# A four-stage transformer kernel: a re-ordered, deeper feed-forward pipeline and moved slots in attention

## The chip, the cores and the metric

The kernel runs on one core of a Trainium2 chip. The metric is the device time of one execution in microseconds (us). The engines are TensorE (PE; PEld is its weight load), VectorE (DVE), ScalarE (ACT), GpSimd (POOL) and SyncE (SP), which issues the DMAs. TensorE's clock has two levels, 1.2 and 2.4 GHz; a granted clock of 1.00 means all of a stretch at the upper one.

## The reference

The input is x of 16 x 256 tokens, 128 features. Four blocks follow each other, each as x = layernorm(x + block(x)): a selective scan (Mamba), a feed-forward part with blockwise FP4 quantization, a differential attention, and a three-layer part with +-1 weights. The change touches the second and the third.

```python
def fp4_quant_dequant(x):            # blocks of 16 along the last dimension
    scale = jnp.maximum(jnp.max(jnp.abs(xb), axis=-1, keepdims=True) / 6.0, 1e-12)
    idx = jnp.searchsorted(_MID, jnp.abs(xb / scale))
    return _GRID[idx] * jnp.sign(xb / scale) * scale
# feed-forward, hidden size 352; x and h are quantized, and the weights too
h = silu(fp4_linear(x, w_gate)) * fp4_linear(x, w_up)
y = fp4_linear(h, w_down)
# attention: q, k rotated; 8 heads with two maps each (16 maps), head dimension 8
o = sdpa(q1, k1, v) - lam * sdpa(q2, k2, v)
o = (o * rsqrt(mean(o**2) + eps) * ln_w + ln_b) * (1 - LAMBDA_INIT)
y = o @ Wo.T
```

## The kernel before

`x_all` keeps all 32 tiles of 128 tokens in SBUF. The stages run one after the other: `mamba_phase`, `ffn_phase`, `attention_phase`, `mlp_phase`. In each one every engine has its own instruction stream, written out by hand in order; semaphores tie them together. So an instruction that waits holds back everything behind it on its engine.

**Feed-forward** (`ffn_phase`). Eight groups of four tiles (512 tokens). A group passes: quantize x (DVE: block maximum, scale, reciprocal, correction, product, L122 to L130; ACT: absolute value, L816; DVE: "magic" maximum and product, L144; POOL: add and subtract the magic number, L149 and L151, which rounds; DVE: multiply by the scale, L156), turn x on PE (L909) and copy it (L847), gate and up projections per tile (L874, L875), silu (L823), product `hidden` (L753), quantize h the same way on 1408 columns instead of 512, turn h (L884), copy (L841, L843), residual (L897) and down projections (L890) into the PSUM tile `dn`, statistics (L81, L86), deviation on POOL (L799), shift (L770), normalize on ACT (L830). `body(n)` on each engine is one step. It mixes group n (gate, up, product, scaling of h), group n+1 (quantization of x) and group n-1 (h back-scaled, turned, projected down, statistics). The scales are in SBUF. Steps 0 to 8 or 9 run, 2 to 6 of them as a hardware loop (`blocks`).

**Attention** (`attention_phase`). One step handles one batch row's scores (two tiles, 16 maps), in 16 slots `u`. In each slot PE makes the scores of map u of group n (`scores`) and two maps' products for the row maximum of a later group (`maxima`), DVE takes the maximum (`row_max`, L1109), and ACT the exponential (L1296). `DELAY` says in which slot the first maximum of group n+2 falls. All other work of groups n-3 to n+5 is hung on slots. The chain that feeds q and k: rotate on POOL, turn on PE (slot 0, L1406), two copies on ACT (L1302, L1304), remainder on POOL (L1232), second part on ACT (L1313), third part on POOL (L1240), parts to DRAM by SP (L1063), back as rows of `qs` and `ks` (L1075, L1078; semaphore `q_in`), awaited by `maxima` with i = 0. The negative maxima are split in three by `split_max`, turned (L1423), copied (L1318, `nmT`) and sent as three rows of `qs` (L1067). SP issues, in this order: parts, the rows of maxima, the loads of q and k.

Of the kernel before, what the change touches and what calls it, by code (L numbers as in the profile page):

```python
# [21 lines left out]
P = 128  # L22
# [633 lines left out]
def ffn_phase(nc, k):  # L656
# [3 lines left out]

    HB = HID // QB
    HC = [(c * P, min(P, HID - c * P)) for c in range((HID + P - 1) // P)]
    ctx = ExitStack()
    with ctx:
# [10 lines left out]
        qh = Quant(sb, sem, "qh", GT * HB)  # L677
# [3 lines left out]
        xqT = sb("xqT", [P, GTOK])  # L681
        sg = sb("sg", [P, GT, HID])
        hid = sb("hid", [P, GT, HID])
        hqT = sb("hqT", [P, 2, len(HC), P])
        stats = sb("stats", [P, GT, 6])
        mv = sb("mv", [P, GT, 2])
        veps = sb("veps", [P, GT])
        rstd = sb("rstd", [P, GT])
# [4 lines left out]
        tx = ps("tx", [P, 512])  # L693
        th = [ps(f"th{i}", [P, 512]) for i in range(2)]
        dn = ps("dn", [P, GT, DM])

        w_turned = sem("w_turned")
        w_copied = sem("w_copied")
        x_turned = sem("x_turned")
# [3 lines left out]
        hid_ready = sem("hid_ready")  # L703
        h_turned = sem("h_turned")
        h_copied = sem("h_copied")
        down_ready = sem("down_ready")
        shift_ready = sem("shift_ready")
        stat_chain = sem("stat_chain")
        rstd_ready = sem("rstd_ready")
        norm_chain = sem("norm_chain")  # L710

        def blocks(eng, body, first=-1):
            for n in range(first, 2):
                body(n)
            with eng.Fori(2, GROUPS - 1) as n:
                body(n)
            for n in range(GROUPS - 1, GROUPS + 2):
                body(n)

        def has(n, lag):  # L720

            return not isinstance(n, int) or 0 <= n + lag < GROUPS
# [9 lines left out]

# [13 lines left out]
        @block.vector  # L746
        def _(dve):
            quant_back(nc, dve, qx, 0)

            def hidden(n, j):  # L750
                if has(n, 0):
                    dve.wait_ge(silu_ready, GT * n + j + 1)
                    nc.vector.tensor_tensor(hid[:, j], sg[:, j], up[j % 2][:, 0:HID], ALU.mult).then_inc(hid_ready, 1)  # L753

            def body(n):
                if has(n, 1):
                    quant_scale(nc, dve, k, qx, ffn_blocks(k, n + 1), n + 1)
                hidden(n, 0)
                if has(n, 1):
                    quant_magic(nc, dve, qx, n + 1)  # L760
                hidden(n, 1)
                hidden(n, 2)
                hidden(n, 3)
                if has(n, -1):
                    wait(dve, h_turned, GT * (n - 1))
                    quant_back(nc, dve, qh, n - 1)
                if has(n, -2):
                    m = n - 2
                    dve.wait_ge(rstd_ready, m + 1)
                    nc.vector.scalar_tensor_tensor(out=shift[:], in0=mv[:, :, 0], scalar=-1.0, in1=rstd[:],  # L770
                                                   op0=ALU.mult, op1=ALU.mult).then_inc(shift_ready, 1)
                if has(n, 0):
                    dve.wait_ge(hid_ready, GT * n + GT)
                    quant_scale(nc, dve, k, qh, hid[:].rearrange("p a (b e) -> p (a b) e", e=QB), n)
                if has(n, 1):
                    wait(dve, x_turned, n + 1)
                    quant_back(nc, dve, qx, n + 1)
                if has(n, 0):
                    quant_magic(nc, dve, qh, n)
                if has(n, -1):  # L780
                    m = n - 1
                    wait(dve, norm_chain, m)
                    dve.wait_ge(down_ready, GT * m + GT)
                    layer_norm_stats(dve, nc, dn, stats, mv, veps, stat_chain, 3 * m)
                    nc.vector.tensor_scalar(veps[:], mv[:, :, 1], LN_EPS, None, ALU.add).then_inc(stat_chain, 1)

            blocks(dve, body, 0)
            dve.wait_ge(norm_chain, GROUPS)

        @block.gpsimd  # L790
        def _(pool):
            def body(n):
                if has(n, 1):
                    quant_middle(nc, pool, qx, n + 1)
                if has(n, 0):
                    quant_middle(nc, pool, qh, n)
                if has(n, -1):
                    pool.wait_ge(stat_chain, 3 * (n - 1) + 3)
                    nc.gpsimd.tensor_tensor(rstd[:], veps[:], k.neg_half[:, 0:GT], ALU.pow).then_inc(rstd_ready, 1)  # L799

            blocks(pool, body, 0)

        @block.scalar
        def _(act):

            for n, dst in enumerate((wgT, wuT)):
                act.wait_ge(w_turned, n + 1)
                nc.scalar.activation(dst[:], (gp[0], up[0])[n][:, 0:HID], ACT.Copy).then_inc(w_copied, 1)
            act.wait_ge(w_turned, 3)
            for c, (_, rows) in enumerate(HC):  # L810
                last = nc.scalar.activation(wdT[0:rows, c, :], tx[0:rows, P * c:P * c + P], ACT.Copy)
            last.then_inc(w_copied, 1)

            def absolute(q, m):
                act.wait_ge(q.front, 6 * m + 5)
                nc.scalar.activation(q.magic[:], q.xs, ACT.Abs).then_inc(q.absolute, 1)  # L816

            def body(n):
                if has(n, 0):
                    for j in range(GT):  # L820
                        act.wait_ge(up_ready, GT * n + j + 1)
                        wait(act, hid_ready, GT * (n - 1) + j + 1)
                        nc.scalar.activation(sg[:, j], gp[j % 2][:, 0:HID], ACT.Silu).then_inc(silu_ready, 1)  # L823
                        if j == 0 and has(n, 1):
                            absolute(qx, n + 1)
                if has(n, -2):
                    m = n - 2
                    act.wait_ge(shift_ready, m + 1)
                    for j in range(GT):
                        last = nc.scalar.activation(k.x_all[:, bass.ds(GT * m + j, 1), :].rearrange("p a b -> p (a b)"),  # L830
                                                    dn[:, j], ACT.Identity, scale=rstd[:, j:j + 1], bias=shift[:, j:j + 1])
                    last.then_inc(norm_chain, 1)
                if has(n, 0):
                    absolute(qh, n)
                if has(n, -1):
                    for j in range(GT):
                        act.wait_ge(h_turned, GT * (n - 1) + j + 1)
                        wait(act, down_ready, GT * (n - 1) + j - 1)
                        src = th[j % 2][:, 0:len(HC) * P].rearrange("p (c t) -> p c t", c=len(HC))
                        full = len(HC) - 1  # L840
                        nc.scalar.activation(hqT[:, j % 2, 0:full], src[:, 0:full], ACT.Copy)  # L841
                        rows = HC[-1][1]
                        nc.scalar.activation(hqT[0:rows, j % 2, full], src[0:rows, full], ACT.Copy).then_inc(h_copied, 1)  # L843
                if has(n, 1):
                    act.wait_ge(x_turned, n + 2)
                    wait(act, up_ready, GT * (n + 1))
                    nc.scalar.activation(xqT[:], tx[:], ACT.Copy).then_inc(x_copied, 1)  # L847

            blocks(act, body)

        @block.tensor
        def _(pe):
# [8 lines left out]
            for c, (at, rows) in enumerate(HC):  # L861
                a = 2 * len(HC) * DM + at
                last = nc.tensor.transpose(tx[0:rows, P * c:P * c + P], wq[:, a:a + rows], ident)
            last.then_inc(w_turned, 1)
            pe.wait_ge(w_copied, 3)

            def body(n):
                if has(n, 0):
                    pe.wait_ge(x_copied, n + 1)
                    for j in range(GT):  # L870
                        wait(pe, silu_ready, GT * n + j - 1)
                        wait(pe, hid_ready, GT * n + j - 1)
                        xt = xqT[:, P * j:P * j + P]
                        nc.tensor.matmul(gp[j % 2][:, 0:HID], xt, wgT[:], start=True, stop=True)  # L874
                        nc.tensor.matmul(up[j % 2][:, 0:HID], xt, wuT[:], start=True, stop=True).then_inc(up_ready, 1)  # L875
                if has(n, -1):
                    m = n - 1
                    pe.wait_ge(qh.back, m + 1)
                    hq = qh.out.rearrange("p (a b) e -> p a (b e)", a=GT)

                    def turn(j):
                        wait(pe, h_copied, GT * m + j - 1)
# [1001 lines left out]
```

## Time and profile before

| | us |
|---|---|
| median of 3 runs (1236.98 to 1244.79) | 1238.01 |
| profiled execution, its own time | 1237.58 |
| its span | 1235.8 |
| PE / DVE / POOL / ACT busy in the span | 968.2 / 942.1 / 818.5 / 720.7 |
| mean granted clock | 0.894 |

The span counts from the first to the last instruction. Mamba fills it up to about 503 us, the feed-forward part up to about 703, attention up to about 1073, and the last part the rest. A busy share says how much an engine worked, not what held it up; for that one reads the waits and the timeline. Times in the timeline are from the span's start.

### The profile page before, as it was taken

The numbers are of one execution on the slowest core, as the hardware profiler recorded it, in microseconds if no ns is written. First come the engines' busy times: TensorE is split into PE (matmuls) and PEld (weight loads), VectorE is DVE, ScalarE is ACT, GpSimd is POOL, SyncE is SP. The second block draws the span as 40 slices with busy tenths as digits, with TensorE's granted clock in tenths as the row PEclk, the third lists the DMA queues.
The fourth block names the chain that finished last, engine by engine and source line by source line (L and its number), as shares of the span: only waits on it lengthen the run. The fifth ranks groups of instructions, "written<-read, shape, count | busy, mean of one in ns | idle before, by whom it ended". The sixth has DMA issues, their size and how long they took to land. (4 is left out here: it accounts for less than half of the span.)

```text
span 1235.8 us, 15659 instructions
## 1 busy us (share of the span) xinstructions
PE 968.2 (78%) x4332; PEld 486.8 (39%) x4347; DVE 942.1 (76%) x1625; ACT 720.7 (58%) x1406; POOL 818.5 (66%) x747
## 2 busy tenths in 40 slices
PE   5689797979797877466665548898898988489996
PEld 2233343424233322343443424454444543235553
DVE  3799999999999999566565226787677784359996
ACT  3777686868676653323333313776666667278772
POOL 1898989899999997244442354575847643467773
PEclk9899999989899989768787655999989999789998
DMA  5552534424251510600000023332323220000001
GB/s 175 229 240 91 195 128 169 172 103 173 102 207 68 228 47 1 108 15 1 0 0 0 1 80 88 91 105 63 95 64 92 79 79 2 0 1 10 18 9 34
DMA packets 34878, 103.84 MB, mean 84 GB/s; under 512 B 3627, under 2 KB 22443, under 8 KB 23979
## 3 DMA queue, kind: packets, MB, share of 16 engines
q1 hardware_dynamic: 34807, 103.03, 24.2%
q8 instruction: 28, 0.46, 0.1%
q14 instruction: 43, 0.35, 0.1%
HBM read 93.71 MB, written 8.91 MB: 83 GB/s over the span
## 5 line engine op out<-in xcount | busy, mean ns | idle before, releaser
L554 PE MATMUL m_yac<-m_hC,ident 128*128 128x512 f32 x512 | 266.5, 641 | 73.6 <-DVE m_hC L315 46.5
L506 POOL TENSOR_TENSOR m_dBu<-m_du,m_Bt 128x1024 f32<-128x1024 f32 x128 | 299.3, 2356 | 6.5 <-DVE m_dA L306 5.1
L1109 DVE TENSOR_REDUCE a_nm<-a_s 128x2 f32<-128x512 f32 x256 | 170.4, 686 | 95.3 <-PE a_s L1348 89.4
L306 DVE TENSOR_TENSOR_SCAN m_dA<-m_dA,m_dBu 128x512 f32<-128x512 f32 x184 | 221.7, 1219 | 15.1 <-ACT m_dA L444 12.1
L1296 ACT ACTIVATE a_pT<-a_s 128x512 f32<-128x512 f32 x256 | 150.9, 600 | 96.9 <-PE a_s L1348 95.9
L554 PEld LDWEIGHTS m_yac<-m_hC,ident 128*128 128x128 f32 x512 | 93.1, 198 | 225.5 <-issue 105.1
L444 ACT ACTIVATE m_dA<-m_delta,mprm 128x510 f32<-128x510 f32 x256 | 169.4, 675 | 0.3
L1348 PE MATMUL a_s<-ks,qs 72*128 72x256 bf16 x512 | 106.5, 294 | 33.0 <-DMA ks<-parts 22.7
L315 DVE TENSOR_TENSOR m_hC<-m_dA,m_Ct 128x512 f32<-128x512 f32 x184 | 123.3, 670 | 0.0
L516 POOL TENSOR_TENSOR m_hC<-m_hS,m_Ct 128x512 f32<-128x512 f32 x72 | 94.6, 1314 | 31.7 <-DVE m_hS L306 31.5
L1644 POOL TENSOR_TENSOR b_h_rest<-b_h_full,b_h_parts 128x512 f32<-128x512 f32 x64 | 77.2, 1212 | 44.9 <-ACT b_h_parts L1669 36.8
L441 ACT ACTIVATE m_dA<-m_zero 128x2 f32<-128x2 f32 x181 | 30.9, 171 | 127.1 <-DVE m_hC L315 126.8
L1348 PE MATMUL a_s<-qs,ks 99*128 99x256 bf16 x512 | 100.9, 281 | 3.2 <-ACT a_pT L1296 2.7
L306 DVE TENSOR_TENSOR_SCAN m_hS<-m_dA,m_dBu 128x512 f32<-128x512 f32 x72 | 86.8, 1206 | 0.0
L1693 PE MATMUL b_hp<-b_h_parts,b_w 128*128 128x512 bf16 x375 | 86.1, 383 | 0.7
L149 POOL TENSOR_TENSOR f_qh_q<-f_qh_xs,f_qh_magic 128x1408 f32<-128x1408 f32 x8 | 25.3, 3165 | 79.5 <-DVE f_qh_magic L144 79.5
L1348 PE MATMUL a_pv<-a_pT,vx 128*32 128x512 f32 x512 | 71.5, 633 | 0.7 <-ACT a_pT L1296 0.7
L1590 DVE TENSOR_TENSOR b_h_parts<-b_h_rest,b_h_parts 128x512 bf16<-128x512 f32 x64 | 63.5, 997 | 10.8 <-ACT b_h_parts L1674 10.0
L1348 PEld LDWEIGHTS a_s<-ks,qs 72*128 72x128 bf16 x512 | 46.8, 102 | 62.9 <-DVE a_nm L1109 34.3
L1348 PEld LDWEIGHTS a_s<-qs,ks 99*128 99x128 bf16 x512 | 45.0, 100 | 65.8 <-ACT a_pT L1296 51.4
L554 PE MATMUL m_pp<-m_xT,m_wk 128*128 128x512 f32 x128 | 61.3, 624 | 2.1 <-DVE m_wk L351 2.1
L1240 POOL TENSOR_TENSOR a_part<-a_res,a_part 128x512 bf16<-128x512 f32 x16 | 18.5, 1157 | 58.8 <-ACT a_part L1313 58.8
(218 smaller groups left out, 1816.5 us busy)
## 6 DMA issues: line engine op xcount, KB each, us to landing
m_Bt<-bcd SPq DMA_DIRECT2D x32, 1024.0 KB, 5.6
m_Ct<-bcd SPq DMA_DIRECT2D x32, 1024.0 KB, 6.6
qs<-parts SPq DMA_DIRECT2D x16, 576.0 KB
ks<-parts SPq DMA_DIRECT2D x48, 192.0 KB
parts<-a_part SPq DMA_DIRECT2D x32, 192.0 KB, 2.2
out<-x_all SPq DMA_DIRECT2D x8, 256.0 KB, 2.3
mprm<-in_mprm SPq DMA_DIRECT2D x1, 1203.0 KB, 6.6
vx<-in_vrow SPq DMA_DIRECT2D x4, 256.0 KB
```

What stands on the lines that cost most here:

```text
L306: nc.vector.tensor_tensor_scan(out, decay, dBu[:, g % RD], 0.0, ALU.mult, ALU.add).then_inc(scan_ready, 1)
L315: nc.vector.tensor_tensor(hC[:, g % RH], dA[g % RA][:].rearrange("p a b -> p (a b)"), Ct[:, s], ALU.mult).then_inc(hcd_ready, 1)
L444: nc.scalar.activation(dA[g % RA][:, :, 1:SEQ], delta[:, n % 2, c].rearrange("p (a b) -> p a b", a=2)[:, :, 1:SEQ], ACT.Exp, scale=decay[: ...
L506: nc.gpsimd.tensor_tensor(dBu[:, g % RD:g % RD + CH], du[:, n % 2], Bt[:, s].unsqueeze(1).broadcast_to([P, CH, GTOK]), ALU.mult).then_inc( ...
L516: nc.gpsimd.tensor_tensor(hC[:, g % RH], hS[:, on_pool(n, i) % RS], Ct[:, s], ALU.mult).then_inc(hcp_ready, 1)
L554: return nc.tensor.matmul(out, lhsT, rhs, start=start, stop=stop)
L1109: nc.vector.tensor_reduce(nm[:, slot % 2, q, 2 * pair:2 * pair + 2], s1[i % 2][:], AX.X, ALU.max, negate=True).then_inc(max_ready, 1)
L1296: nc.scalar.activation(pT[:, u // 2, u % 2], s2[u % 2][:], ACT.Exp, scale=float(HD) ** -0.25).then_inc(exp_ready, 1)
L1348: return nc.tensor.matmul(out, lhsT, rhs, start=start, stop=stop)
L1590: nc.vector.tensor_tensor(part_tile(s, p, c, 2), rest_tile(s, c), part_tile(s, p, c, 1), ALU.subtract).then_inc(s.low_ready, 1)
L1644: nc.gpsimd.tensor_tensor(rest_tile(s, c), full_tile(s, c), part_tile(s, q, c, 0), ALU.subtract).then_inc(s.rest_ready, 1)
L1693: return nc.tensor.matmul(out, lhsT, rhs, start=start, stop=stop)
```

## The change

The feed-forward part is written out for steps -1 to 10 instead of a loop. h of group n-1 gets its magic number, its rounding and its back-scaling in step n, is turned and projected down in step n+1, and is normalized in step n+2. x is quantized two groups ahead instead of one. The scales and their reciprocals lie in one PSUM bank (`sc`); the x turn shares the bank `th[0]` with the turns of h; `xqT` and the quantized h are double. The epsilon addition and the shift move from DVE to POOL. `scale_x`, `scale_h`, `back_x`, `back_h`, `statistics`, `silu`, `took_h`, `gate_up`, `turn`, `residual`, `down`, `turn_x` hold the same operations as before. In attention the first maximum moves to slot 3, and the work around it to other slots. POOL's third part gets one more wait.

```diff
--- feed-forward, buffers
-        qh = Quant(sb, sem, "qh", GT * HB)
-        xqT = sb("xqT", [P, GTOK])
+        xqT = sb("xqT", [P, 2, GTOK])
+        hxs, hmagic, hq = ...                      # [P, NHB, QB] each
+        hout = sb("hout", [P, 2, NHB, QB])
-        tx = ps("tx", [P, 512])
+        sc = ps("sc", [P, 512])
+        h_scale = [sc[:, NHB * i:NHB * i + NHB] for i in range(2)]
+        h_inv = sc[:, 2 * NHB:3 * NHB]
+        x_scale = sc[:, 3 * NHB:3 * NHB + NXB]
+        x_inv = sc[:, 3 * NHB + NXB:3 * NHB + 2 * NXB]
+        STEPS = range(-1, GROUPS + 3)
--- feed-forward, VectorE
+            def magic_x(m):
+                dve.wait_ge(x_abs, m)
+                nc.vector.tensor_scalar(qx.magic[:], qx.magic[:], 1.0, 2.0 ** 22 + 2.0, ALU.max,
+                                        ALU.mult).then_inc(x_magic, 1)
+            for n in STEPS:
                 hidden(n, 0)
+                if has(n - 1):
+                    magic_h(n - 1)
                 hidden(n, 1)
+                if has(n + 2):
+                    scale_x(n + 2)
                 hidden(n, 2)
+                if has(n + 2):
+                    magic_x(n + 2)
                 hidden(n, 3)
+                if has(n):
+                    scale_h(n)
+                if has(n - 1):
+                    back_h(n - 1)
+                if has(n + 2):
+                    back_x(n + 2)
+                if has(n - 2):
+                    statistics(n - 2)
--- feed-forward, GpSimd
+            for n in STEPS:
+                m = n - 3
+                if has(m):
+                    pool.wait_ge(stat_chain, 2 * m + 2)
+                    nc.gpsimd.tensor_tensor(veps[:], mv[:, :, 1], eps[:], ALU.add).then_inc(rstd_step, 1)
+                    nc.gpsimd.tensor_tensor(nmean[:], mv[:, :, 0], minus[:], ALU.mult).then_inc(rstd_step, 1)
+                    ...
+                    nc.gpsimd.tensor_tensor(rstd[:], veps[:], k.neg_half[:, 0:GT], ALU.pow).then_inc(rstd_step, 1)
+                    pool.wait_ge(rstd_step, 3 * m + 3)
+                    nc.gpsimd.tensor_tensor(shift[:], nmean[:], rstd[:], ALU.mult).then_inc(shift_ready, 1)
+                m = n - 1
+                if has(m):
+                    pool.wait_ge(h_magic, m + 1)
+                    wait(pool, h_back, m)
+                    nc.gpsimd.tensor_tensor(hq[:], hxs[:], hmagic[:], ALU.add).then_inc(h_add, 1)
+                    pool.wait_ge(h_add, m + 1)
+                    nc.gpsimd.tensor_tensor(hq[:], hq[:], hmagic[:], ALU.subtract).then_inc(h_sub, 1)
+                m = n + 2
+                if has(m):
+                    pool.wait_ge(x_magic, m)
+                    ...
--- feed-forward, ScalarE
+            for n in STEPS:
+                silu(n, 0)
+                ...                                # Abs of h, group n - 1
+                silu(n, 1)
+                took_h(n - 2, 0)
+                took_h(n - 2, 1)
+                if has(n - 3):
+                    normalize(n - 3)
+                silu(n, 2)
+                ...                                # Abs of x, group n + 2
+                took_h(n - 2, 2)
+                silu(n, 3)
+                took_h(n - 2, 3)
+                ...                                # x copy, group n + 1
--- feed-forward, TensorE
+            for n in STEPS:
+                gate_up(n, 0)
+                gate_up(n, 1)
+                turn(n - 2, 0)
+                turn(n - 2, 1)
+                gate_up(n, 2)
+                residual(n - 2)
+                down(n - 2, 0)
+                turn(n - 2, 2)
+                down(n - 2, 1)
+                gate_up(n, 3)
+                turn(n - 2, 3)
+                down(n - 2, 2)
+                turn_x(n + 1)
+                down(n - 2, 3)
--- attention
-        DELAY = 2
+        DELAY = 3
--- attention, VectorE: split_max u 2, 3 -> 3, 4; head_norm u 4 -> 5; leave(n - 1, 1) u 6 -> 8; difference u 7 -> 9
--- attention, GpSimd (residual_middle)
+                wait(pool, q_in, 64 * m)
                 wait(pool, x_turned, min_group(m + 2, BATCH))
--- attention, ScalarE
-                    if u == 1 and has(n, 3):       # qkT copy
+                    if u == 0 and has(n, 3):
-                    if u == 2 and has(n, 3):       # first part
+                    if u == 1 and has(n, 3):
-                    if u == 3 and has(n, 4):       # xT copy
+                    if u == 2 and has(n, 4):
-                    if u == 4 and has(n, -1):      # copy_sums(n - 1, 1)
+                    if u == 3 and has(n, -1):
-                    if u == 5 and has(n, 3):       # second part
+                    if u == 4 and has(n, 3):
-                    if u in (7, 9) and has(n, 4):  # qkv copies
+                    if u in (5, 6) and has(n, 4):
-                    if u == 6 and has(n, 1):       # nmT copy
+                    if u == 8 and has(n, 1):
-                    if u == 10 and has(n, -2):     # oT copy
+                    if u == 9 and has(n, -2):
--- attention, TensorE: x turn u 2 -> 1; qkv u 6, 8 -> 4, 5; turn_sums(n - 1, 1) u 5 -> 6; o turn u 9 -> 8; turn of the maxima:
-                    if u == 5 and has(n, 1):
+                    if u == 7 and has(n, 1):
                         pe.wait_ge(nm_chain, 5 * (n + 1) + 5)
-                        wait(pe, xT_ready, min_group(n + 5, BATCH))
+                        wait(pe, qkv_ready, min_group(2 * (n + 5), 2 * BATCH))
```

## Rows read from the trace of the kernel before

**Rows 1.** Windows: stretch, length, busy PE, PEld, DVE, ACT, POOL, granted clock, DMA share, GB/s.

```profile
503.50:524.10 20.60, 12.22 (x33) 7.57 (x33) 11.29 (x21) 7.77 (x14) 2.54 (x2) 0.67 0.87 158
553.60:575.40 21.80, 14.72 (x58) 9.95 (x58) 13.53 (x32) 7.82 (x19) 9.64 (x5) 0.77 0.00 1
642.80:665.80 23.00, 14.78 (x58) 10.73 (x58) 13.41 (x30) 7.83 (x19) 9.89 (x5) 0.78 0.00 0
665.80:702.94 37.14, 21.74 (x92) 15.34 (x92) 14.26 (x41) 11.77 (x33) 10.68 (x5) 0.76 0.00 0
```

**Rows 2.** Waits, feed-forward stage: engine and line, releaser, total us, times, longest.

```profile
DVE f_stats L81 <- PE f_dn L890: 47.0, 8, 8.3
```

**Rows 3.** Windows, two attention steps, columns as in rows 1.

```profile
871.56:890.15 18.59, 16.77 (x129) 9.49 (x128) 15.10 (x36) 13.23 (x28) 13.35 (x24) 1.00 0.30 89
933.06:953.42 20.36, 18.28 (x129) 9.91 (x127) 14.59 (x36) 13.23 (x28) 13.35 (x24) 0.92 0.28 81
```

**Rows 4.** Waits, attention, 760 to 1040 us.

```profile
PE a_s L1348 <- DMA ks<-parts: 16.1, 11, 2.6
```

**Rows 5.** Timeline, one attention step and the load it needs.

```profile
863.15 0.89 SPq L1063 DMA_DIRECT2D parts<-a_part  x2
...
866.05 0.84 SPq L1075 DMA_DIRECT2D qs<-parts  x1
...
875.39 0.39 PE L1348 MATMUL a_s<-ks,qs 72*128 72x256 bf16 x2 [1.47 <-DMA ks<-parts]
...
876.01 1.16 POOL L1232 TENSOR_TENSOR a_res<-a_qkT,a_part 128x512 f32<-128x512 f32 x1
...
879.60 0.66 ACT L1313 ACTIVATE a_part<-a_res 128x512 bf16<-128x512 f32 x1
...
880.72 0.36 ACT L1318 ACTIVATE a_nmT<-a_ma 48x256 bf16<-48x256 bf16 x1
```

**Rows 6.** Timeline, PE: start us, duration us; one low-clock row, three at full clock.

```profile
592.90 1.49 PE L890 MATMUL f_dn<-f_wdT,f_hqT 128*128 128x128 f32 x6
...
598.98 0.76 PE L875 MATMUL f_up<-f_wuT,f_xqT 128*128 128x352 f32 x2
599.57 0.76 PE L874 MATMUL f_gp<-f_wgT,f_xqT 128*128 128x352 f32 x2
...
695.70 0.83 PE L890 MATMUL f_dn<-f_wdT,f_hqT 128*128 128x128 f32 x6
```

**Rows 7.** Timeline, end of the feed-forward stage.

```profile
700.19 1.01 POOL L799 TENSOR_TENSOR f_rstd<-f_veps,neg_half 128x4 f32<-128x4 f32 x1 [10.10 <-DVE f_veps L785]
...
701.43 1.51 ACT L830 ACTIVATE x_all<-f_dn,f_shift,f_rstd 128x128 f32<-128x128 f32 x4 [3.98 <-DVE f_shift L770]
```

**Rows 8.** Groups of the feed-forward stage: busy us, mean ns | idle before, releaser.

```profile
L149 POOL TENSOR_TENSOR f_qh_q<-f_qh_xs,f_qh_magic 128x1408 f32<-128x1408 f32 x8 | 25.3, 3165 | 79.5 <-DVE f_qh_magic L144 79.5
...
L753 DVE TENSOR_TENSOR f_hid<-f_sg,f_up 128x352 f32<-128x352 f32 x32 | 16.6, 520 | 24.4 <-ACT f_sg L823 24.4
...
L130 DVE TENSOR_TENSOR f_qh_xs<-f_hid,f_qh_inv 128x1408 f32<-128x1408 f32 x8 | 13.0, 1626 | 0.3
L156 DVE TENSOR_TENSOR f_qh_out<-f_qh_q,f_qh_scale 128x1408 f32<-128x1408 f32 x8 | 13.0, 1620 | 0.0
L122 DVE TENSOR_REDUCE f_qh_scale<-f_hid 128x88 f32<-128x1408 f32 x8 | 12.9, 1611 | 0.0
...
L144 DVE TENSOR_SCALAR f_qh_magic<-f_qh_magic 128x1408 f32<-128x1408 f32 x8 | 7.2, 894 | 7.3 <-ACT f_qh_magic L816 7.3
...
L144 DVE TENSOR_SCALAR qx_magic<-qx_magic 128x512 f32<-128x512 f32 x7 | 3.0, 427 | 1.6 <-ACT qx_magic L816 1.6
```

**Rows 9.** Timeline, POOL and DVE around 527 us.

```profile
527.34 3.15 POOL L151 TENSOR_TENSOR f_qh_q<-f_qh_q,f_qh_magic 128x1408 f32<-128x1408 f32 x1
527.72 2.80 DVE L128 TENSOR_SCALAR qx_inv<-qx_inv 128x32 f32<-128x32 f32 x1
```

**Rows 10.** Timeline, PE, the first load of the attention stage.

```profile
731.76 0.61 PE L1348 MATMUL a_s<-ks,qs 72*128 72x256 bf16 x2 [5.24 <-DMA ks<-parts]
```

More of the change, by code:

```diff
@@ L791, in _ @@
         def _(pool):
[L792 to L801, printed above, removed]
+            pool.wait_ge(const_ready, 2)
@@ L806, in _, with normalize @@
+            def normalize(m):
+                act.wait_ge(shift_ready, m + 1)
+                for j in range(GT):
+                    last = nc.scalar.activation(k.x_all[:, GT * m + j, :], dn[:, j], ACT.Identity,
+                                                scale=rstd[:, j:j + 1], bias=shift[:, j:j + 1])
+                last.then_inc(norm_chain, 1)
             for n, dst in enumerate((wgT, wuT)):
@@ L810, in _ @@
             for c, (_, rows) in enumerate(HC):
-                last = nc.scalar.activation(wdT[0:rows, c, :], tx[0:rows, P * c:P * c + P], ACT.Copy)
+                last = nc.scalar.activation(wdT[0:rows, c, :], th[1][0:rows, P * c:P * c + P], ACT.Copy)
             last.then_inc(w_copied, 1)
[L814 to L847, printed above, removed]
@@ new lines, in turn @@
+            def turn(m, j):
+                if has(m):
+                    if j == 0:
+                        pe.wait_ge(h_back, m + 1)
+                        wait(pe, x_copied, min(m + 3, GROUPS))
+                    wait(pe, h_copied, GT * m + j - 1)
+                    src = hout[:, m % 2].rearrange("p (a b) e -> p a (b e)", a=GT)
+                    for at, rows in HC:
+                        last = nc.tensor.transpose(th[j % 2][0:rows, at:at + P], src[:, j, at:at + rows], ident)
+                    last.then_inc(h_turned, 1)
@@ L904, in body, with down @@
-                if has(n, 1):
-                    pe.wait_ge(qx.back, n + 2)
-                    wait(pe, x_copied, n + 1)
-                    xq = qx.out.rearrange("p (a b) e -> p a (b e)", a=GT)
-                    for j in range(GT):
-                        last = nc.tensor.transpose(tx[:, P * j:P * j + P], xq[:, j], ident)
-                    last.then_inc(x_turned, 1)
-            blocks(pe, body)
+            def down(m, j):
+                if has(m):
+                    pe.wait_ge(h_copied, GT * m + j + 1)
+                    for c, (_, rows) in enumerate(HC):
+                        last = nc.tensor.matmul(dn[:, j], hqT[0:rows, j % 2, c], wdT[0:rows, c],
+                                                start=False, stop=(j == GT - 1 and c == full))
+                    last.then_inc(down_ready, 1)
```

257 lines of the change are left out of this document (160 added, 97 removed).

## The prediction

> **What bounds the kernel now.** I read the views in this order: the windows by stage, then the waits of the feed-forward stage, then one of its steps in the timeline, then one attention step.
>
> The feed-forward stage runs from 503.5 to 702.94, 199.4 us for eight groups. In a steady step no engine is full. In 21.8 to 23.0 us DVE is busy 13.5, PE 14.7 (at a granted clock of 0.77), POOL 9.7, ACT 7.8 [rows 1]. So a chain bounds it, not a resource. The wait that shows it is DVE's for the last down projection, 47.0 us in 8 times [rows 2]: one step holds, in series, quantize, turn, down, turn of x, gate and up, product. The last stretch, 37.1 us, is the last group's tail alone [rows 1].
>
> An attention step takes 18.59 us with PE busy 16.8 at full clock, or 20.36 where the clock was 0.92 [rows 3]. PE is the bound, with one hole: at the first maximum of a group it waits for the q and k load (here 1.47 us), 16.1 us over 11 steps [rows 4, 5]. 18.59 less 1.47 is 17.1: a step without the hole. The closing multilayer stage is untouched.
>
> **Feed-forward, what an engine has to do.** The two more pipeline steps put the quantization of h, its down projection and its norm into three different steps. Work per step hardly changes. DVE loses two one-element copies, the epsilon addition and the shift (estimate 0.6 us) and pays about as much again for scales that now lie in PSUM (estimate: between 0 and 0.1 us for each of eight operations). I keep 13.5. POOL takes over three tiny operations. PE's calls at full clock: gate and up of one tile 1.18 (two starts 0.59 apart), a down 0.75 (0.83 less its overlap), a turn 0.42, the residual 0.85, the x turn 0.6 [rows 6] (the last three estimated from their columns), in all 4.7 + 3.0 + 1.7 + 0.85 + 0.6 = 10.9; at the low level (1.2 GHz) 22, as the same six down matmuls take 1.49 against 0.83 [rows 6].
>
> **Feed-forward, which chain sets the period.** Two loops go from one statistics call to the next:
> - *Loop A, POOL's long pair.* Statistics, POOL's four operations for the deviation (pow 1.01, the other three 0.2 each with waits: 1.75) [rows 7], DVE's h magic 0.89, POOL's add and subtract 3.17 and 3.16, DVE's x magic 0.43, the last product 0.52, and then what DVE does behind it. That last is 13.5 less four products (2.1), the h magic, the x magic and the scaling of x (estimate 2.1): 8.0 [rows 1, 8]. Sum 17.9, with some eight handovers of 0.1: 18.8.
> - *Loop B, PE's.* 1.75, normalize 1.51 [rows 7], residual 0.85, down, turn, down (1.9), gate and up of the last tile 1.18, silu 0.47, product 0.52, then the same 8.0: 16.2, with handovers 17.0. At the low level the PE part grows from 4.0 to 8, and it is 21.
>
> Loop A rests on a behaviour of the trace. A DVE tensor-with-scalar operation on 32 columns took 2.80 us, from 527.72 to 530.52, because POOL's subtraction held until 530.49 [rows 9]; one on 1408 columns takes 0.89 when it is free [rows 8]. The x magic is of this kind, and in the new order it arrives just as POOL begins the subtraction of h. Were it not held, A would lose 2.9 us and B would decide. The change puts the scales into PSUM, so only the two magic operations are still of this kind.
>
> The Trainium skill ("SBUF — State Buffer", section "Who interferes with whom") says that DVE in a two-port mode and GpSimd exclude each other for a whole instruction, and that a DVE operation with two SBUF inputs also contends with a GpSimd read. By the first, the trace agrees. It speaks against the placing of the x magic, and without it the steady step would be 17.0 instead of 18.8.
>
> PE's clock comes between. In one loop PE now has gaps of about 2.5, 1.8 and 1.7 us in a row (waiting for the h back-scaling, the first product, the normalization), much like the pauses behind which today's steps fall to the low level (mean 0.77). So I expect the loop's PE part to begin low and end high: 19.5 us for steps 3 to 5, halfway between 18.8 and 21 and nearer the former. Steps 6 and 7 have no x to quantize, which removes A: B without the x work is 16.3 to 20.3, taken as 18.3.
>
> **Feed-forward, the sum.** Start: step -1 8 us (weights turned and copied, x group 1), step 0 13 (four tiles at the low level, as in the first window), step 1 16.5, step 2 17.5 (no normalization yet): 55. Steady: 3 x 19.5 + 2 x 18.3 = 95. End: after the last product POOL's pair for h and back-scaling, statistics of group 6 (12 us), normalize, eight turns and downs (10.2), statistics, deviation, normalize (5): 27. Together 177 against 199.4: **-22 us**. Both-fast end: 53 + 3 x 18.8 + 2 x 16.3 + 26 = 168, -31. All-low end: 55 + 3 x 22 + 2 x 20.5 + 31 = 193, -6. Fetching the unrolled steps instead of a loop I cost at nothing (mean of a gain and a loss I can't see); bounds +-2.
>
> **Attention.** The chain of the load, counted from slot 0 (871.12, 0.44 before the window of [rows 3]) with the hole of 1.47 taken out: the second part's copy on ACT begins at 7.0 today (879.60), behind the exponential of slot 5 [rows 5]. One slot earlier it could begin at 5.5, but POOL's remainder ends at 877.17, that is 6.05 [rows 5], so about 6.2. POOL's 1.16 follows, and the parts go out at 8.05 instead of 9.1. The q load is issued 2.9 us behind [rows 5], at 11.0. There the change meets its own other edit: SP sends the rows of maxima first, and these now come off ACT in slot 8 instead of 6, at about 10 instead of 8.5; with their 1.9 us of issue the q load leaves at about 12.1. It lands, as now, 9.3 us behind its issue (866.05 to 875.39) [rows 5], at 21.4. It is needed at slot 3 of the next step: today's place 2.7 us into a step, and then a weighted call of 1.0, the x turn and two small pairs, 4.5; 17.1 + 4.5 = 21.6. So the hole of about 1.4 us shrinks to 0 to 0.5. Against this, ACT waits some 0.7 us for the remainder in slot 4, and PE some 0.3 for ACT in slot 7, where it now needs the second qkv copy. Net -1.0 per step, 12 steps: -12. While the pipeline fills, PE's wait of 5.24 us for the first load [rows 10] no longer stands ahead of the x turn (slot 1, not 2): the second load leaves up to 4 us sooner, of which I count 1. POOL's new wait for the earlier loads is over at 4.4 us into the step, 2.5 before it is reached: nothing; if loads came later it would delay the parts by as much. The later slots of head norm, leaving and difference have their consumers at least one slot behind: nothing. Sum **-13**, bounds -20 (hole gone, no new wait) and 0 (below).
>
> **Sum.** 1237.6 - 22 - 13 = 1202.6. The profiled execution took 1237.58 (span 1235.8), 0.4 below the median of 1238.01, so against the median 1203; I say 1203.
>
> **Rivals.**
> - *The attention load only moves* (18%). The rows of maxima hold SP longer than I think, since PE turns them only after ACT's slot-6 copy. A delay of 1.5 us there restores the hole. For: that order is new, and the margin is 0.2 us. Against: everything else in the chain is earlier. Attention -1, total 1214.
> - *Feed-forward at the high clock* (18%): -31 and -13, 1193.
> - *Loop B at the low clock for most steps* (17%): -6 and -13, 1218. For: today's 0.77 with PE busy 65% of a step.
> - *Slower* (5%): PE stays at 1.2 GHz through the feed-forward part. Its 22 us of calls plus 3 us of in-order waits give 25 a step; 60 + 5 x 25 + 33 = 218, +19. With the hole unfilled as well the total is 1255. It decides against the change from (199.4 - 93)/5 = 21.3 us a step where attention gives nothing. Against: the granted clock is never below 0.76 in the steady windows [rows 1], and PE would be denser.
> - *No effect* (5%): a chain I have not seen keeps the step at 22 us, as the two added steps then eat the gain of the tail: within 1%.
>
> The Trainium skill ("TensorE: Matmul & The Clock Gate", section "HAM oscillation — how this bites in real kernels") says that a kernel with repeated pauses on PE oscillates between the two levels. By that rule the low-clock case would be the likelier one; the windows here with 0.77 agree with oscillation.
>
> **Numbers.** Forecast 37%, rivals as given. The range is 1186 to 1222: the high-clock case at its lower end, the low-clock case at its upper, with both bounds of attention. A measurement of this kernel can tell about 1% from no change. Faster by over 1% (below 1225.6): 37 + 18 + 18 + 17, less 4 for the tails of these: 86%. Within 1%: 10%. Slower: 4%.
>
> **What would show it.** Right: a feed-forward stage of about 177 us with steady steps of 19.5; an x magic operation that takes 2 to 3.5 us instead of 0.43, ending when POOL's subtraction ends; attention steps near 17.5 with PE's wait for the load under 0.5. Wrong: an x magic at 0.43 and steps of 17 (loop A is no loop), steady steps above 21 with DVE waiting for a late gate product (loop B low), or an unchanged hole at slot 3 with SP waiting for the rows of maxima.

## The result and the profile after

The changed kernel takes 1173.47 us (median of 4 runs, 1172.86 to 1179.49) against 1237.49 for the kernel before on the same chip: ratio 0.949 [0.945, 0.953], 64 us faster. The forecast was 1203 with a range of 1186 to 1222, so the gain is almost twice the one forecast and the time lies below the range. The direction was right, the size wrong.

The profiled execution (1173.17 us, span 1171.4) splits as follows; "before" is the same cut of the span of 1235.8.

| stage | before | after | difference | forecast |
|---|---|---|---|---|
| feed-forward, 503.6 to the first x turn of attention | 200.9 | 159.7 | -41.2 | -22 |
| attention, to the first turn of the last part | 368.9 | 346.4 | -22.5 | -13 |
| the last part | 162.4 | 161.7 | -0.7 | 0 |

Windows of the feed-forward stage after, columns as in [rows 1], cut at the first product of each step (steps 0, 1, 2, 3, 4, 5, 6, 7 and the end):

```profile
511.20:521.91 10.71, 6.42 (x23) 3.46 (x21) 9.39 (x17) 3.34 (x7) 2.54 (x2) 1.00 0.93 139
521.91:534.66 12.75, 7.97 (x24) 4.56 (x25) 11.76 (x19) 5.52 (x9) 9.11 (x4) 0.87 0.36 57
534.66:550.94 16.28, 12.76 (x62) 8.82 (x60) 13.05 (x28) 7.40 (x19) 9.11 (x4) 0.90 0.00 1
550.94:567.75 16.81, 12.61 (x58) 8.28 (x58) 13.03 (x27) 7.81 (x19) 10.40 (x8) 0.90 0.00 0
567.75:584.68 16.93, 13.19 (x58) 8.76 (x58) 13.03 (x28) 7.54 (x18) 10.39 (x8) 0.83 0.00 0
584.68:601.68 17.00, 13.47 (x58) 9.01 (x58) 13.06 (x27) 7.92 (x20) 10.40 (x8) 0.80 0.01 2
601.68:618.11 16.43, 13.21 (x58) 9.00 (x58) 10.04 (x20) 6.78 (x18) 7.80 (x6) 0.81 0.00 0
618.11:634.86 16.75, 11.01 (x48) 7.30 (x46) 10.04 (x20) 5.88 (x17) 7.79 (x6) 0.70 0.00 1
634.86:661.50 26.64, 14.44 (x72) 11.31 (x70) 5.17 (x20) 8.33 (x28) 11.50 (x14) 0.76 0.00 0
```

Steps 3, 4 and 5 are the steady ones; steps 6 and 7 have no x left to quantize. A steady step takes 17 us, not the 22 to 23 of [rows 1], with nearly the same DVE time in it (13.0). The granted clock is 0.80 to 0.90 in the steady steps and 0.70 to 0.81 in steps 6 and 7, against 0.77 and 0.78 in the steps of [rows 1]. The two waits that bounded or could bound the step, feed-forward stage after:

```profile
DVE f_hid L768 <- ACT f_sg L892: 25.7, 9, 4.3
...
DVE f_stats L81 <- PE f_dn L994: 10.5, 2, 9.7
```

The second is the 47.0 us of [rows 2], now left almost only in the tail. DVE waited for silu before too, 24.4 us in all [rows 8], but spread over 20 short waits; now it is one long wait a step, for the silu of the last tile. One step of the timeline after, put in the order of time, shows what the silu waits for:

```profile
550.94 0.52 DVE L768 TENSOR_TENSOR f_hid<-f_sg,f_up 128x352 f32<-128x352 f32 x1
...
551.29 1.03 POOL L868 TENSOR_TENSOR f_rstd<-f_veps,neg_half 128x4 f32<-128x4 f32 x1
...
551.38 0.89 DVE L819 TENSOR_SCALAR f_hmagic<-f_hmagic 128x1408 f32<-128x1408 f32 x1
...
552.54 3.17 POOL L875 TENSOR_TENSOR f_hq<-f_hxs,f_hmagic 128x1408 f32<-128x1408 f32 x1
...
552.63 1.50 ACT L906 ACTIVATE x_all<-f_dn,f_shift,f_rstd 128x128 f32<-128x128 f32 x4 [1.97 <-POOL f_shift L870]
...
553.33 0.20 DVE L776 TENSOR_SCALAR f_sc<-f_sc 128x32 f32<-128x32 f32 x1
...
554.18 1.57 PE L986 MATMUL f_dn<-x_all,ident 128*128 128x512 f32 x2
...
555.59 0.43 DVE L788 TENSOR_SCALAR qx_magic<-qx_magic 128x512 f32<-128x512 f32 x1 [0.27 <-ACT qx_magic L935]
...
555.79 3.24 POOL L877 TENSOR_TENSOR f_hq<-f_hq,f_hmagic 128x1408 f32<-128x1408 f32 x1
...
556.59 0.83 PE L994 MATMUL f_dn<-f_wdT,f_hqT 128*128 128x128 f32 x6
...
557.26 0.76 PE L968 MATMUL f_gp<-f_wgT,f_xqT 128*128 128x352 f32 x2
...
558.65 0.46 ACT L892 ACTIVATE f_sg<-f_gp 128x352 f32<-128x352 f32 x1 [1.31 <-PE f_up L969]
...
559.14 0.52 DVE L768 TENSOR_TENSOR f_hid<-f_sg,f_up 128x352 f32<-128x352 f32 x1 [3.13 <-ACT f_sg L892]
```

This is loop B of the prediction: deviation, normalize, residual, down projections, gate and up of the last tile, silu, last product, and then 8.1 us of DVE to the next step at 567.75. The x magic starts at 555.59, 0.12 us before POOL's addition ends (555.71) and 0.20 before its subtraction starts (555.79), and takes 0.43 us, in this step and in the six others that have one (426 to 428 ns). So nothing holds it. It is POOL that is held a little: the subtraction takes 3.24 to 3.26 us in steps 3 to 5, and 3.17 and 3.16 in steps 6 and 7, which have no x magic. In steps 1 and 2 there is no margin to speak of; step 1:

```profile
527.05 0.43 DVE L788 TENSOR_SCALAR qx_magic<-qx_magic 128x512 f32<-128x512 f32 x1 [0.27 <-ACT qx_magic L935]
527.06 3.44 POOL L877 TENSOR_TENSOR f_hq<-f_hq,f_hmagic 128x1408 f32<-128x1408 f32 x1
```

The two records start within 0.01 us of each other, here and in step 2 (539.30 and 539.29); the magic keeps its 0.43, and the subtraction is 0.3 us longer than usual (3.44 and 3.45). The h magic runs beside POOL's pow (551.29 to 552.32); I had put one behind the other.

Attention after. PE's waits for row maxima and for the load (11 steps, 734 to 930 us), one step, and SP's transfers of that step:

```profile
PE a_s L1458 <- DVE a_nm L1217: 9.3, 18, 0.9
PE a_s L1458 <- DMA ks<-parts: 2.4, 3, 1.2
```

```profile
840.89:858.12 17.23, 16.38 (x128) 9.49 (x127) 14.95 (x36) 13.20 (x28) 13.67 (x24) 1.00 0.31 91
```

```profile
849.32 0.90 SPq L1171 DMA_DIRECT2D parts<-a_part  x2
850.95 1.82 SPq L1175 DMA_DIRECT2D qs<-a_nmT  x3
852.91 0.85 SPq L1183 DMA_DIRECT2D qs<-parts  x1
```

The 16.1 us of [rows 4] are 2.4, and the step of 18.59 [rows 3] is 17.23 with PE busy 16.38. What PE waits for in these steps is now mostly DVE's row maxima, 9.3 us. Over the whole attention stage the waits for the load fell from 22.7 to 9.8 us. The load of q leaves 12.5 us behind slot 0 (840.45), as forecast (12.1), because the rows of maxima stand ahead of it in SP's queue and come 10.5 us in.

### The profile page after: what moved, and what is told of

Read it like the earlier page. It is cut to its first block and busy times, and to the rows that moved or that the text cites. A ratio compares the mean times of both kernels' runs of the same rounds, so it can differ in the third digit from the quotient of the medians.

```text
span 1171.4 us, 15467 instructions
## 1 busy us (share of the span) xinstructions
PE 938.8 (80%) x4332; PEld 470.9 (40%) x4347; DVE 940.0 (80%) x1597; ACT 720.2 (61%) x1406; POOL 824.9 (70%) x771
## 5 line engine op out<-in xcount | busy, mean ns | idle before, releaser
L554 PE MATMUL m_yac<-m_hC,ident 128*128 128x512 f32 x512 | 261.1, 629 | 76.2 <-DVE m_hC L315 47.6
L306 DVE TENSOR_TENSOR_SCAN m_dA<-m_dA,m_dBu 128x512 f32<-128x512 f32 x184 | 221.4, 1217 | 15.0 <-ACT m_dA L444 12.1
L1458 PE MATMUL a_s<-ks,qs 72*128 72x256 bf16 x512 | 104.1, 288 | 24.7 <-DVE a_nm L1217 14.4
L306 DVE TENSOR_TENSOR_SCAN m_hS<-m_dA,m_dBu 128x512 f32<-128x512 f32 x72 | 86.6, 1203 | 0.0
L1458 PE MATMUL a_pv<-a_pT,vx 128*32 128x512 f32 x512 | 69.0, 613 | 0.7 <-ACT a_pT L1406 0.7
L1458 PEld LDWEIGHTS a_s<-ks,qs 72*128 72x128 bf16 x512 | 44.3, 101 | 56.5 <-DVE a_nm L1217 36.9
L554 PE MATMUL m_pp<-m_xT,m_wk 128*128 128x512 f32 x128 | 63.9, 646 | 2.1 <-DVE m_wk L351 2.1
L1777 ACT ACTIVATE b_h_parts<-b_h_full 128x512 bf16<-128x512 f32 x64 | 40.2, 629 | 26.3 <-DVE b_h_full L1718 23.2
L1801 PEld LDWEIGHTS b_hp<-b_h_parts,b_w 128*128 128x128 bf16 x384 | 37.0, 98 | 45.9 <-issue 3.3
```

The source lines that it names most:

```text
L306: nc.vector.tensor_tensor_scan(out, decay, dBu[:, g % RD], 0.0, ALU.mult, ALU.add).then_inc(scan_ready, 1)
L554: return nc.tensor.matmul(out, lhsT, rhs, start=start, stop=stop)
L1458: return nc.tensor.matmul(out, lhsT, rhs, start=start, stop=stop)
L1801: return nc.tensor.matmul(out, lhsT, rhs, start=start, stop=stop)
```

## The experiments

**1 and 2. Each half alone.** `att_only`: the feed-forward part of before and the attention of after. `ffn_only`: the reverse.

```diff
--- att_only (attention_phase of after stays)
- ffn_phase of after
+ ffn_phase of before
--- ffn_only (ffn_phase of after stays)
- attention_phase of after
+ attention_phase of before
```

The experiments ran on other chips than the result, each beside the kernel before; so whole times are best compared by their ratio to it. Stage times below come from the profiled executions; the feed-forward stage is counted from its first turn of the weights, which came between 503.6 and 507.0 us.

> The feed-forward part of before with the attention part of after. If the two halves of the change add up, as the two traces suggest (attention 368.9 us before, 346.4 after), it takes about 1237.5 - 22.5 = 1215 us and its attention part 346 to 347 us. If part of the attention gain came with the new feed-forward part (another state of the clock or of the instruction queues at the stage's start), it stays above 1220 us. My forecast for this half had been -13, that is 1224.

> The feed-forward part of after with the attention part of before. If the halves add up: 1237.5 - 41.2 = 1196 us, attention part 369 us, with the same holes of 1.3 to 2.6 us before the first row maximum and the same VectorE hole of about 4 us at the back edge of the attention loop. If the 4 us hole was an accident of one execution, it is missing here and the time is 1192 us.

Measured: `att_only` 1224.27 us, ratio 0.988 [0.983, 0.993]; `ffn_only` 1199.91, ratio 0.968 [0.964, 0.973]; before 1241.09. So 17 and 41 us, 58 of the 64. The feed-forward gain is there with the old attention: its stage takes 160.0 us against 159.7. The attention gain alone is smaller than in the full change: 354.5 us for the stage against 346.4. One row is as long as half of that, a wait of DVE for nothing that the profile shows. It stands at the step in which the hardware loop of attention goes round for the first time. In `att_only`, then in the kernel before:

```profile
888.47 1.29 DVE L1109 TENSOR_REDUCE a_nm<-a_s 128x2 f32<-128x512 f32 x2 [4.34 <-issue]
```

```profile
895.87 1.29 DVE L1109 TENSOR_REDUCE a_nm<-a_s 128x2 f32<-128x512 f32 x2 [3.88 <-issue]
```

Neither the changed kernel nor `ffn_only` has it. Between the two kernels with the hole, attention gains 14.4 us (368.9 to 354.5); between the two without it, 23.0 (369.4 to 346.4). But the old attention takes the same time with the hole (368.9) as without it (369.4), so the hole cannot be subtracted as a fixed cost. More on this under 8.

**3. The x magic made late.** `late_magic` puts one more DVE operation ahead of it, so that it arrives inside POOL's subtraction.

```diff
+                    nc.vector.tensor_reduce(late[:, n + 1:n + 2], k.wts[:, 0:512], AX.X, ALU.max)
                     magic_x(n + 2)
```

> After, with one extra VectorE maximum over 512 SBUF columns (0.69 us) ahead of the magic operation of x, so that this arrives inside GpSimd's subtraction of h and not at the seam between its addition and subtraction. Theory A (a two-port VectorE operation waits for the whole GpSimd operation): the magic operation takes about 3 us instead of 0.43 in steps 3 to 5, ending with the subtraction, and the steps grow by 0.3 to 0.6 us only, since VectorE waited 3.2 us for the last silu there anyway; in steps 1 and 2, where it did not wait (or 2.6 us), they grow by 2.5 and 0.5. Sum +4 to +5: about 1178 us. Rival B (no such lock; the long 32-column operation of before was something else): magic stays at 0.43, and only the extra 0.69 us counts where VectorE did not wait: +1, 1174.5 us.

Measured: 1185.71, ratio 0.956 [0.952, 0.960]. The timeline, POOL's subtraction and the x magic in one step:

```profile
560.72 3.15 POOL L879 TENSOR_TENSOR f_hq<-f_hq,f_hmagic 128x1408 f32<-128x1408 f32 x1
560.76 3.40 DVE L789 TENSOR_SCALAR qx_magic<-qx_magic 128x512 f32<-128x512 f32 x1
```

0.43 us became 3.40: the behaviour on which loop A rested is real. In the changed kernel the magic missed it by 0.2 us, here it starts 0.04 us behind POOL. But the steps hardly grew: 16.64, 16.95 and 17.0 against 16.28, 16.81 and 16.93; only step 1, in which loop B has no down projection yet, grew by 3.0. So even with the hold, A is no longer than B. The run is above the 1178 expected. Between the two profiled executions lie 10.1 us: the feed-forward stage has 4.2 of them, attention 4.4, where the same hole of DVE stands again (4.25), and 1.0 lies ahead of both.

**4. The scales back in SBUF.** `sbuf_scales`: all else as after.

```diff
-        sc = ps("sc", [P, 512])
+        ss = sb("ss", [P, 3 * NHB + 2 * NXB])
```

> After, with the block scales and their reciprocals in SBUF instead of PSUM. Theory A: the scale operations of x (on 32 columns) then wait for GpSimd's addition and subtraction of h in turn, as at 527.72 us in the trace of before; the scaling of x ends about 4.5 us later, magic of x after the subtraction, and the last product about 2 us later than today. Steps 1 to 5 grow from 12.8 to 17 to about 17 to 19.5, sum +12 us: 1185 us. Rival B: nothing changes but the 0.06 us that each small PSUM operation costs more: 1171 to 1173 us.

Measured: 1192.44, ratio 0.961 [0.956, 0.966]; steady steps of 18.6 to 19.3, the stage 172.5 us, 12.8 longer. Timeline, one step:

```profile
543.69 3.16 POOL L876 TENSOR_TENSOR f_hq<-f_hxs,f_hmagic 128x1408 f32<-128x1408 f32 x1 [6.16 <-DVE f_hmagic L820]
...
544.67 2.22 DVE L777 TENSOR_SCALAR f_ss<-f_ss 128x32 f32<-128x32 f32 x1
...
546.93 3.16 POOL L878 TENSOR_TENSOR f_hq<-f_hq,f_hmagic 128x1408 f32<-128x1408 f32 x1
547.31 2.81 DVE L781 TENSOR_SCALAR f_ss<-f_ss 128x32 f32<-128x32 f32 x1
```

Two operations of 0.20 us in PSUM take 2.22 and 2.81, each to the end of one POOL operation. The new order needs the scales in PSUM, and the move is worth 13 us of the 41.

**5. Loop B shortened.** `early_gate` takes the last tile's gate and up from behind the residual and two down projections to ahead of them.

```diff
--- TensorE
                 gate_up(n, 2)
+                gate_up(n, 3)
                 residual(n - 2)
                 down(n - 2, 0)
                 turn(n - 2, 2)
                 down(n - 2, 1)
-                gate_up(n, 3)
--- ScalarE
-                took_h(n - 2, 2)
                 silu(n, 3)
+                took_h(n - 2, 2)
```

> After, with gate and up of the last tile ahead of the residual on TensorE, and its silu ahead of the third copy of h on ScalarE. Theory (the steady step of 16.9 us is the loop over statistics, deviation, normalize, residual, two downs, gate and up, silu, last product; VectorE waits 3.1 to 3.3 us there): the last product no longer waits, and VectorE's own 13.0 us of work with its hand-overs decides, so steps 2 to 7 take 13.5 to 14 us: -3.2 us in five or six steps, 1156 us. Rival: another wait takes its place, above all VectorE's statistics for the last down projection or its x back-scaling for GpSimd (10.4 us of work in a step), and a step takes 15.5 us or more: 1166 us.

Measured: 1157.38 us (1154.05 to 1158.24), ratio 0.931 [0.926, 0.936]. The feed-forward stage takes 140.3, a step 13.6, except one. Three windows of it, columns as in [rows 1]:

```profile
538.43:552.12 13.69, 12.69 (x63) 8.95 (x61) 13.06 (x29) 7.26 (x19) 9.13 (x4) 0.88 0.00 0
552.12:565.73 13.61, 10.98 (x58) 7.64 (x58) 12.97 (x28) 7.70 (x19) 10.41 (x8) 0.99 0.01 1
565.73:580.56 14.83, 13.50 (x58) 9.42 (x58) 13.06 (x27) 7.20 (x18) 10.40 (x8) 0.78 0.00 0
```

DVE is busy 13.0 of 13.6: the chain is gone and an engine is the bound. This shows that B set the 17 us of the changed kernel. In the step of 14.83 the granted clock was 0.78, all four matmul pairs before the last silu ran at the lower level (1.38 to 1.51 us a pair, not 0.76), and DVE waited 1.16 us for that silu. The kernel beats both others.

**6 and 7. The two edits of attention apart.** `delay_only` keeps the first maximum in slot 3 and puts the rest of attention back to its old slots; `chain_only` keeps the new slots and puts the maximum back to 2.

```diff
delay_only (attention; DELAY = 3 stays)
-                    if u in (3, 4) and has(n, 1):      # split_max
+                    if u in (2, 3) and has(n, 1):
-                    if u == 4 and has(n, 3):           # second part
+                    if u == 5 and has(n, 3):
-                    if u == 8 and has(n, 1):           # nmT copy
+                    if u == 6 and has(n, 1):
...
chain_only
-        DELAY = 3
+        DELAY = 2
```

> The feed-forward part of after, the attention part of before with DELAY = 3 and GpSimd's new wait for the loads, all other slots as before. In both attention parts the q load leaves 12.1 to 12.5 us into a step and lands 9.3 us later; so theory A (slot 3 alone fills the hole, the shorter chain brings nothing, as the rows of maxima gate the load) gives holes of 0 to 0.3 us and steps of 17.2 to 17.5: about 1183 us, 17 below the kernel with the whole attention part of before, the rest of the gain (2 to 3 us while the pipeline fills) missing. Rival B (both edits are needed, half of it each): 1190 us with holes of 0.7 us.

> After with DELAY = 2: the shorter q and k chain, but the first row maximum in slot 2 again. Theory A: the load is needed 1.5 us sooner and leaves no sooner than before, so the holes are 1.5 to 2 us and the steps 18.6 to 19: 1173 + 12 x 1.5 = 1191 us. Rival B: the shorter chain has half of the gain, holes of 0.7 us, 1182 us.

Measured: `delay_only` 1182.67, ratio 0.952 [0.947, 0.957], attention 352.3 and steps of 17.9 with no wait for the load once the pipeline is full. `chain_only` 1202.77, ratio 0.968 [0.963, 0.973], attention 378.9, which is 9.5 more than the old attention in `ffn_only`. PE's wait over 200 us (760 to 960), in `chain_only`, then in `ffn_only`:

```profile
PE a_s L1458 <- DMA ks<-parts: 21.2, 10, 3.1
```

```profile
PE a_s L1456 <- DMA ks<-parts: 17.1, 10, 2.7
```

So slot 3 removes the waits, and the new slots without it make them longer, since they send the maxima two slots later and the load of q stands behind these on SP: it left 14.7 us into the step at 841.50 in `chain_only`, and 12.4 us into the step at 855.91 in `ffn_only`. These waits are 4.1 of the 9.5 us. The rest goes along with the clock: 9 of 11 steps of `chain_only` (738.6 to 959.0 us) ran at a granted clock of 0.85 to 0.92, against 5 of 11 in `ffn_only`. I had expected 1191 of `chain_only`. Together with slot 3 the new slots are worth 6 us (352.3 to 346.4).

**8. The hole in attention.** `late_written_out` is `late_magic` with the attention steps written out.

```diff
-            for n in range(-5, FIRST):
-                body(n, n % RING)
-            with eng.Fori(0, (LAST + 1 - FIRST) // RING) as i:
-                ...
+            for n in range(-5, BATCH + 3):
```

> The kernel with the delayed x magic, its attention steps written out instead of a hardware loop over four steps. That kernel's trace has a VectorE hole of 4.25 us at the loop's one back edge (put down to issue), as those of before and of the kernel with the attention part alone, while after and two others have none. If the back edge causes it (instructions fetched anew behind the jump), it is gone and the time falls by about 4 us to 1181.5 us. If not, it stays or moves: 1185.7 us.

Measured: 1189.97, ratio 0.958 [0.953, 0.963], where I had expected at most 1185.7. The hole is gone, so it belongs to the loop's turn; but attention grew from 350.8 to 358.2, steps of 18.1 at full clock and of 19.4 at a granted clock of 0.91 in turn. DVE's groups from 770 to 910 us say where, first `late_magic`, then `late_written_out`:

```profile
L1254 DVE SCALAR_TENSOR_TENSOR a_o<-a_av,a_neg_lam 128x256 f32<-128x256 f32 x8 | 6.5, 806 | 0.0
...
L1235 DVE TENSOR_TENSOR a_nmr<-a_nmr,a_nmp 128x32 f32<-128x32 f32 x7 | 2.3, 330 | 0.2
```

```profile
L1249 DVE SCALAR_TENSOR_TENSOR a_o<-a_av,a_neg_lam 128x256 f32<-128x256 f32 x8 | 12.0, 1505 | 0.0
L1230 DVE TENSOR_TENSOR a_nmr<-a_nmr,a_nmp 128x32 f32<-128x32 f32 x7 | 8.0, 1146 | 0.2
```

The same operations take 1.50 instead of 0.81 and 1.15 instead of 0.33 us. In the step at 817 us the second stands beside POOL's `a_part` (start 817.92, 1.16 long) and ends with it, as in experiment 4. So with the loop written out DVE's operations meet POOL's at other places, and more of them are held. DVE is busy 17.0 us in the steps of 18.1, against 15.0 to 15.7 in the steps of 17.0 to 17.6 of `late_magic`; the other 1.3 us of every second step come with the lower clock. That the holds make the difference between 17.0 to 17.6 and 18.1 is argued from these rows, not tried. Why the two engines stay in this order wasn't tried.

**9. Late magic with loop B short.** `early_late`: `early_gate` with the extra operation of experiment 3.

> Edit: early_gate (the gate/up products of tile 3 ahead of the residual's, which ran at 1157.4 us) with one VectorE maximum over 512 columns (about 0.6 us) ahead of the magic division of x, in the six steps that have one; its result is used by nobody. Theory A (VectorE's two-port operations can't run beside GpSimd's two-port ones, first come holds): x's magic now arrives inside GpSimd's subtraction and takes 2.5 to 3.5 us instead of 0.43, as in late_magic; there the longer operation fell into slack of the loop through TensorE and steps 3 to 6 grew by less than 0.2 us. Here that loop is shorter (steps of 13.6), so the operation and its wait sit on the loop: each of about five steps grows by 2 to 3 us, the feed-forward stage from 142.9 to 153 to 157, the run to about 1169 (1166 to 1173). Rival B (no lock; the extra operation costs only its own time): steps grow by 0.6 to 0.7, the stage by about 3.5, the run to 1161. Rival C (the loop of this order runs through other work, so that the magic division has slack): steps unchanged, 1157 to 1158.

Measured: 1177.77, ratio 0.951 [0.949, 0.954]. Timeline, one step:

```profile
560.06 3.17 POOL L879 TENSOR_TENSOR f_hq<-f_hq,f_hmagic 128x1408 f32<-128x1408 f32 x1
560.10 3.41 DVE L789 TENSOR_SCALAR qx_magic<-qx_magic 128x512 f32<-128x512 f32 x1
...
563.43 0.51 DVE L769 TENSOR_TENSOR f_hid<-f_sg,f_up 128x352 f32<-128x352 f32 x1
```

The hold of 3 us now costs: steps of 16.8 instead of 13.6, the stage 156.5 instead of 140.3 (the 142.9 of the expectation was counted from 503.6 us, 2.5 too early for that run). The stage lies within the 153 to 157 expected. The run is 5 us above the highest of my range, 1173; 3.74 of that is as long as the hole of DVE, which is back. With B out of the way, this is loop A with the hold: 16.8 us, where I had 18.8. The extra 0.68 us is not in it: it runs beside POOL's pair, ahead of the magic, whose end the subtraction sets.

## Why the prediction was wrong

Miss by term, in us: the start of the feed-forward stage 8; its steps 3 to 7 together 11; its end 0; attention 9.5. Every term that missed was too long; none alone makes the miss.

- **The step that failed: "Loop A", 18.8 us with the x magic held until POOL's subtraction ends.** The x magic took 0.43 us and A set nothing. I had it arrive "just as POOL begins the subtraction" and took it for late, without a margin. It came 0.19 to 0.20 us early in steps 3 to 5, and within 0.01 us of the subtraction in steps 1 and 2, and was held in none; so on which side of the subtraction's start it would fall could not be told from my sum, whose handovers alone were eight of 0.1. Experiments 3 and 9 show that the hold exists, and that A with it is 16.8: the sum was 2 us too long as well. Of these 0.9 is the h magic, which I had put behind POOL's pow and which ran beside it (0.89 us at 551.38, pow to 552.32), and most of the rest the handovers. So the steady step should have been loop B's 17.0; B's total was priced right (16.81, 16.93, 17.00), and experiment 5 shows that it was the bound. That the total fits so well is in part luck: the slow residual added some 0.6 us, and the handovers added less than the 0.8 allowed. Loop A's 18.8 instead of 17.0 is 5.4 of the 11 us; with 17.0 the forecast would have been 1198, still far too high. The prediction had this case as a sign of being wrong ("steps of 17"), but no rival of its own: the nearest, the high-clock rival, gave 1193, still 20 us too high, since it has loop A's 18.8 in it too.
- **The allowance for the clock.** Halfway to a low-clock B of 21 I took 19.5, and 18.3 for steps 6 and 7; measured 16.4 and 16.75. The granted clock did fall, to 0.80 to 0.90. By the timeline of the step, the slow calls (gate and up of tile 2, 1.42 and 1.38 us, and the residual, 1.57) lie mostly beside POOL's and ACT's part of the loop; only the residual is in it. The Trainium skill ("TensorE: Matmul & The Clock Gate", section "HAM oscillation — how this bites in real kernels") speaks of such a change between levels. The windows show it (0.70 to 0.90), and by its rule the low-clock case would have been the likelier one; its time did not come. That the clock can cost where the slow calls are on the path shows in experiment 5, 14.83 us at 0.78 against 13.6 at 0.99. Allowance and loop A together are the 11 us: 7.8 in steps 3 to 5, 3.4 in steps 6 and 7.
- **Start: 55 us forecast, 47.4 measured** (7.6, 10.7, 12.75, 16.3 for steps -1 to 2, against 8, 13, 16.5, 17.5). I gave step 0 the low clock of the first window of [rows 1]; it had 1.00. Step 1 I took nearly as a full one; but it has neither a normalization nor an h to project, so no loop binds it, and DVE is busy 11.8 of 12.75.
- **End: 27 forecast, 26.6 measured.** Right. The two added steps did not eat the gain.
- **Attention: -13 forecast, -22.5 measured, -14.4 in `att_only`.** The mechanism was right, to the position of the q load (12.1 and 12.5) and the wait that is left (2.4 us over 11 steps). The sizes were off: the wait of 0.3 at ACT's copies did not show (0.4 in 11 steps), the waits for the load fell by 12.9 us over the stage, and against the kernel before the hole of 3.9 us at the loop's turn is gone. Steps at a granted clock of 0.91 to 0.92 were 4 of 11 before (778 to 991 us) and 1 of 11 after; the one after took 19.1 us against 17.2 and 17.5 beside it. These three overlap, and how the 22.5 divides among them the runs here don't show. "The load only moves" was wrong: experiment 6 shows that the slot alone frees PE. But the transfer ahead of the load that this rival named, the rows of maxima on SP, lengthened the waits of `chain_only` against the old order.
- **The range.** Its upper end, 1222, is not what its sentence says: the low-clock case with the upper bound of attention, 0, gives 1237.6 - 6, that is 1232. Its lower end, 1186, holds loop A's 18.8. The time fell below the range, so only the second mattered.

## What to carry to other kernels

When two loops of a pipelined stage come out within 2 us of each other, place every operation of both on one time axis before adding a hold between engines: an arrival 0.2 us earlier decides whether it costs 3 us or nothing, and a margin smaller than the errors of the sum calls for both cases as forecasts with a chance each. After a change has balanced two loops, look for the work in the longer one that needn't be there: moving the gate and up matmuls of one tile ahead of the residual took 19 us more from the stage, until DVE was full. And a shorter chain to a transfer brings nothing while another transfer, later than it, stands ahead in the same queue; moving the consumer did.

## What the runs showed of the hardware

- A DVE tensor-with-scalar operation in SBUF that arrives during a POOL operation ends with it: 0.43 us became 3.40 and 3.41, 0.20 became 2.22 and 2.81. With its data in PSUM the operation on 32 columns takes 0.20 beside the same POOL addition (553.33, in the changed kernel). The Trainium skill ("SBUF — State Buffer", section "Who interferes with whom") has DVE in a two-port mode and GpSimd exclude each other for a whole instruction; these rows agree. Where the two started within 0.01 us of each other (steps 1 and 2 of the changed kernel), DVE's kept its 0.43 us and POOL's subtraction took longer, 3.44 and 3.45 us instead of 3.17. The last 0.12 us of POOL's addition (555.59 to 555.71) did not hold it either. One row does not fit: the h magic of the same kind took its usual 0.89 us beside POOL's pow on 4 columns (1.03 us).
- At the first turn of a hardware loop of four unrolled attention steps DVE stood 3.7 to 4.3 us in the kernel before, `att_only`, `late_magic` and `early_late`, and not in the others, though the attention code of `late_magic` and of the changed kernel is the same; written out, there was none. What decides it stays open, and so does its cost in the whole: the old attention took 368.9 us with it and 369.4 without. Its step took 22.9 us against 17.5 for the one before it, with the granted clock at 0.85 against 1.00 (`att_only`); it can pass for the effect of an edit elsewhere.
